# Starting the scatters of typed rows bank by bank, inside the stages that compute the rows

## The reference, cut to what matters

```python
x = _layernorm(x + _L2_gnn_ref(x, ...), axis=-1)
x = _layernorm(x + _L3_gnn_ref(x, node_type_16, edge_type_32, src, dst, ...), axis=-1)

def typed_linear(x, t, W):                      # each node by the matrix of its type
    y_all = jnp.einsum('nd,tdo->nto', x, W)     # 16 types
    return jnp.take_along_axis(y_all, t[:, None, None], axis=1)[:, 0]

def gt_layer(x, ntype, etype, src, dst, Wk, Wq, Wv, Wa, Watt, Wmsg, pri, skip, g, b):
    k, q, v = typed_linear(x, ntype, Wk), typed_linear(x, ntype, Wq), typed_linear(x, ntype, Wv)
    ...                                         # keys and values by edge type, scores, softmax, messages
    h = silu(typed_linear(hag, ntype, Wa))
    h = h * alpha + x * (1.0 - alpha)
    return (h - mean(h)) * rsqrt(var(h) + 1e-05) * g + b

h = x
for l in range(2):
    h = gt_layer(h, ...)
return h @ ff_w + ff_b
```

## Time and profile before

| | |
|---|---|
| Median of 3 runs | 6942.57 us (6941.76 to 6949.24) |
| The profiled execution's own time | 6940.74 us |
| Its span, in which all positions in the trace are told | 6937.9 us |
| Busy: TensorE, VectorE, ScalarE, GpSimd | 49%, 33%, 16%, 46% |
| Mean granted TensorE clock | 0.647 of full speed |

### The profile page before, as it was taken

The page is one execution under the profiler, slowest core; times in us unless marked ns, Lnnn a source line. Parts: engine busy times, 40 slices in busy tenths (PEclk is TensorE's granted clock), DMA queues, the critical chain, the costliest instruction groups (busy, mean ns, idle before and its releaser), DMA issues. The chain is left out here.

```text
span 6937.9 us, 64367 instructions
## 1 busy us (share of the span) xinstructions
PE 3401.2 (49%) x15913; PEld 2652.2 (38%) x15913; DVE 2282.3 (33%) x5027; ACT 1115.3 (16%) x2358; POOL 3195.3 (46%) x3405
## 2 busy tenths in 40 slices
PE   2566567646774555743363334633433446244344
PEld 2565445434453555532233232223333322233243
DVE  5222222222223222411121114523337535233385
ACT  0000122222222001200010001410103424011043
POOL 1666356635662565166636663045540230555302
PEclk8555577777776555655575556766666767566676
DMA  1111133323432232211131115954442479444333
GB/s 41 43 46 46 40 94 99 100 68 93 100 100 78 73 85 84 97 43 46 47 120 43 46 43 210 426 163 122 122 116 85 138 275 426 116 123 122 106 115 109
DMA packets 600942, 772.38 MB, mean 111 GB/s; under 512 B 89734, under 2 KB 507000, under 8 KB 588064
## 3 DMA queue, kind: packets, MB, share of 16 engines
q1 hardware_dynamic: 480000, 492.16, 21.3%
q0 software_dynamic: 120608, 276.12, 14.9%
HBM read 416.10 MB, written 351.82 MB: 111 GB/s over the span
## 5 line engine op out<-in xcount | busy, mean ns | idle before, releaser
L396 POOL DMA_INDIRECT arena<-table,idx_s x3128 | 2973.1, 950 | 2753.8 <-issue 867.9
L633 PE MATMUL ps<-arena,onehot 128*128 x4160 | 1067.3, 399 | 772.3 <-issue 483.1
L633 PEld LDWEIGHTS ps<-arena,onehot 128*128 128x128 f32 x4160 | 854.8, 284 | 921.0 <-issue 920.3
L374 DVE TENSOR_TENSOR onehot<-ps,dl_s 128x512 f32<-128x512 f32 x520 | 351.4, 686 | 1391.7 <-remote 1026.2
L1813 PE MATMUL ps<-ident,onehot 128*128 128x128 f32 x832 | 192.0, 374 | 658.4 <-DVE onehot L374 492.5
L1773 DVE TENSOR_TENSOR arena<-arena,ps 128x128 f32<-128x128 f32 x832 | 183.9, 282 | 845.2 <-remote 642.1
L803 DVE SCALAR_TENSOR_TENSOR arena<-ps,vecs,arena 128x256 f32<-128x256 f32 x208 | 100.6, 484 | 971.4 <-issue 617.2
L1824 PE MATMUL ps<-arena 128*128 x1664 | 330.5, 363 | 153.4 <-issue 108.7
L1813 PEld LDWEIGHTS ps<-ident,onehot 128*128 128x128 f32 x832 | 136.1, 194 | 688.8 <-DVE onehot L374 508.1
L1824 PEld LDWEIGHTS ps<-arena 128*128 128x128 f32 x1664 | 298.1, 269 | 182.7 <-issue 179.9
L1693 PE MATMUL ps<-arena,XT 32*128 32x512 f32 x1600 | 307.0, 900 | 97.1 <-DVE XT L1717 48.5
(11 more groups left out here) (327 smaller groups left out, 4520.8 us busy)
## 6 DMA issues: line engine op xcount, KB each, us to landing
table<-arena SPq DMA_DIRECT2D x96, 2048.0 KB
values<-arena SPq DMA_DIRECT2D x832, 64.0 KB
arena<-values SPq DMA_DIRECT2D x208, 256.0 KB
arena<-table,idx_s POOLq DMA_INDIRECT x3128
arena<-edge_times SPq DMA_DIRECT2D x208, 128.0 KB
edge_part<-arena SPq DMA_DIRECT2D x208, 128.0 KB
table<-arena SPq DMA_DIRECT2D x50, 512.0 KB
arena<-edge_part SPq DMA_DIRECT2D x98, 256.0 KB
```

The costliest lines, as they stand in the source:

```text
L374: is_dst = dve.tensor_tensor(onehot[:, 4 * q:4 * q + 4, :], iota.unsqueeze(1).to_broadcast([P, 4, P]), dl_s[:, ds(j, 4)].unsqueeze(2).to_b ...
L396: pool.indirect_dma_start(ring[:, ds(t % RING * 2 * H, width)], None, tab, bass.IndirectOffsetOnAxis(ap=idx_s[:, t:t + 1], axis=0)).then_i ...
L633: mm = pe.matmul(accf[:, ds(b, P)], o, ring[:, ds(slot, H)], start=False, stop=False, skip_group_check=True)
```

## The change

Four edits:

1. The scatters of the keys/values/queries product leave `by_type_phase`. For layer 0 they stand in the stage ahead of it, each bank of 4 behind a wait on `scaled`, and read `Xn`. For layer 1 they stand in the last stage of layer 0, behind that stage's 25 gathers, each bank behind a wait on `rows_ready`, which VectorE now raises in both layers.
2. The loads of weights, `Watt`, `Wmsg` and `pri` move with them, on semaphores of their own (`weighed`, `paired`). A few small tiles of the last stage get other places in `arena`, since the weights now lie where they stood.
3. `residual_norm_phase` and the small copying stage ahead of layer 0 become one stage. The addition, mean, squares and scaling are done bank by bank with the helpers that other stages use, and squares are summed on ScalarE.
4. The copy to `Lx` moves from GpSimd to ScalarE, bank by bank.

The typed product on the messages (`heard=True`) keeps its scatters and loads where they were.

```diff
-            residual_norm_phase(lambda ch, dve: ch(dve.tensor_tensor(Xn[:, :, :], Xn[:, :, :], acc_nodes, ALU.add)))
...
+            def place_rows(pool, src, b):
+                pool.indirect_dma_start(sorted_x, bass.IndirectOffsetOnAxis(ap=pos_i[:, b:b + 1], axis=0),
+                                        src[:, b, :], None).then_inc(placed.sem, 16)
+
+            def type_loads(sp, weights, layer):
+                C = len(weights) * H
+                wall = type_w[:, 0:NT * C].rearrange("p (t c) -> p t c", t=NT)
+                for w, W in enumerate(weights):
+                    sp.dma_start(wall[:, :, w * H:(w + 1) * H], W.rearrange("t f o -> f t o")).then_inc(weighed.sem, 16)
+                if layer is not None:
...
 def by_type_phase(src, weights, sorted_y, layer=None, heard=False):
-                    @block.gpsimd
-                    def _(pool):
-                        for b in range(NB):
-                            if heard and b % 4 == 0:
...
+                    if heard:
+                        @block.gpsimd
+                        def _(pool):
+                            for b in range(NB):
...
+                        if heard:
+                            type_loads(sp, weights, layer)
                         sp.wait_ge(placed.sem, placed.at(16 * NB))
...
                 if l == 0:
                     with nc.Block() as block:
+                        square = arena[:, 10000:10000 + NP].rearrange("p (b f) -> p b f", f=H)
+                        @block.sync
+                        def _(sp):
+                            type_loads(sp, kvq_weights[0], 0)
                         @block.gpsimd
                         def _(pool):
-                            pool.tensor_copy(Lx[:, :, :], Xn[:, :, :])
+                            for b in range(NB):
+                                if b % 4 == 0:
+                                    pool.wait_ge(scaled.sem, scaled.at(b // 4 + 1))
+                                place_rows(pool, Xn, b)
+                        @block.scalar
+                        def _(act):
+                            for k in range(BANKS):
+                                act_squares(act, k, Xn, k + 1, square)
+                            act_root(act, 1)
+                            for k in range(BANKS):
+                                c = slice(span(k)[2][0], span(k)[2][-1] + 1)
+                                act.wait_ge(scaled.sem, scaled.at(k + 1))
+                                act.activation(Lx[:, c, :], Xn[:, c, :], ACT.Copy)
                         @block.vector
                         def _(dve):
                             ch = Chain(dve, vdone)
+                            for k in range(BANKS):
+                                a, e, blocks = span(k)
+                                c = slice(blocks[0], blocks[-1] + 1)
+                                ch(dve.tensor_tensor(Xn[:, c, :], Xn[:, c, :], accf[:, a:e].rearrange("p (b f) -> p b f", f=H), ALU.add))
+                                dve_mean(ch, dve, k, Xn, red)
+                            dve_deviation(ch, dve, BANKS, 1)
+                            for k in range(BANKS):
+                                dve_scale(dve, k, Xn)
                             ch(dve.scalar_tensor_tensor(w1_f, src_s[:, 0:TILES], float(T32), t32_s[:, 0:TILES], ALU.mult, ALU.add))
                             ch(dve.tensor_copy(idx_s[:, 0:TILES], w1_f))
```

In the last stage of a layer, on GpSimd behind the 25 gathers, on SyncE behind the four small loads, and on VectorE per bank:

```diff
+                        if not last:
+                            for b in range(NB):
+                                if b % 4 == 0:
+                                    pool.wait_ge(rows_ready.sem, rows_ready.at(b // 4 + 1))
+                                place_rows(pool, Lx, b)
...
+                        if not last:
+                            type_loads(sp, kvq_weights[1], 1)
...
-                            if last:
-                                dve.sem_inc(rows_ready.sem, 1)
-                                if k >= 2:
-                                    output(k - 2)
+                            dve.sem_inc(rows_ready.sem, 1)
+                            if last and k >= 2:
+                                output(k - 2)
```

More of the change, by code:

```diff
@@ L190, in build @@
         produced = signal("produced")
+        weighed = signal("weighed")
+        paired = signal("paired")
         cube = arena[:, 0:STEPS * NB]
@@ L1514, in build @@
             join = arena[:, 20600:20600 + LINKS + 1]
[L1515 to L1518, removed]
+            alpha = arena[:, 23200:23200 + NB]
+            types_n = arena[:, 23240:23240 + NB].bitcast(I32)
+            skip_bc = arena[:, 23280:23280 + NT]
+            eq_types = arena[:, 23300:23300 + NB * NT].rearrange("p (b t) -> p b t", t=NT)
             vals = arena[:, 7600:7600 + U * H].rearrange("p (r f) -> p r f", r=U)
@@ L1535, in kvq @@
                 return arena[:, 18700 + (b - 16) * 3 * H:18700 + (b - 15) * 3 * H]
+            def place_rows(pool, src, b):
[7 more added lines that the diff above has]
+                if layer is not None:
+                    sp.dma_start(raw[:, 0, :, :].rearrange("p t o -> p (t o)"), A["L3_Watt"][layer]).then_inc(paired.sem, 16)
+                    sp.dma_start(raw[:, 1, :, :].rearrange("p t o -> p (t o)"), A["L3_Wmsg"][layer]).then_inc(paired.sem, 16)
+                    for h in range(HEADS):
+                        sp.dma_start(pri[h * HS:(h + 1) * HS, :], A["L3_gnn_pri"][layer, h].partition_broadcast(HS)).then_inc(paired.sem, 16)
             def by_type_phase(src, weights, sorted_y, layer=None, heard=False):
@@ L1543, in by_type_phase @@
                 extra = 2 + HEADS if layer is not None else 0
-                flat_src = src[:, :, :].rearrange("p b f -> p (b f)")
+                flat_src = src[:, :, :].rearrange("p b f -> p (b f)") if heard else None
                 with nc.Block() as block:
-                    @block.gpsimd
-                    def _(pool):
-                        for b in range(NB):
-                            if heard and b % 4 == 0:
[L1550 to L1553, removed]
+                    if heard:
[3 more added lines that the diff above has]
+                                if b % 4 == 0:
+                                    k = b // 4
+                                    pool.wait_ge((mixed if k % 2 == 0 else squared).sem, (mixed if k % 2 == 0 else squared).at(k // 2 + 1))
+                                place_rows(pool, src, b)
                     @block.sync
                     def _(sp):
[L1557 to L1563, removed]
+                        if heard:
+                            type_loads(sp, weights, layer)
                         sp.wait_ge(placed.sem, placed.at(16 * NB))
@@ L1589, in _ @@
                         turn(0)
-                        pe.wait_ge(loaded.sem, loaded.at(16 * len(weights)))
+                        pe.wait_ge(weighed.sem, weighed.at(16 * len(weights)))
                         for g in range(GROUPS):
@@ L1623, in _ @@
                             ch(dve.tensor_reduce(pair_mask, head_mask[:, :].rearrange("p (a j) -> p j a", j=2), AX.X, ALU.add))
-                            dve.wait_ge(stored.sem, stored.at(16 * extra))
+                            dve.wait_ge(paired.sem, paired.at(16 * extra))
                             ch(dve.tensor_tensor(raw[:, 0, :, :], raw[:, 0, :, :], pri.unsqueeze(2).to_broadcast([P, T32, HS]), ALU.mult))
@@ L1637, in _ @@
                             dve.tensor_copy(out_ring[:, g % 6, c, :], ps[:, 2 + n % 6, 0:C]).then_inc(copied.sem, 1)
-                loaded.base += 16 * len(weights)
-                stored.base += 16 * extra
+                weighed.base += 16 * len(weights)
+                paired.base += 16 * extra
                 placed.base += 16 * NB
@@ L2021, in build @@
             for l in range(2):
+                kvq_weights = [[A["L3_gnn_Wk"][n], A["L3_gnn_Wv"][n], A["L3_gnn_Wq"][n]] for n in range(2)]
                 if l == 0:
                     with nc.Block() as block:
+                        square = arena[:, 10000:10000 + NP].rearrange("p (b f) -> p b f", f=H)
+                        @block.sync
+                        def _(sp):
+                            type_loads(sp, kvq_weights[0], 0)
                         @block.gpsimd
                         def _(pool):
-                            pool.tensor_copy(Lx[:, :, :], Xn[:, :, :])
+                            for b in range(NB):
[11 more added lines that the diff above has]
+                                act.activation(Lx[:, c, :], Xn[:, c, :], ACT.Copy)
                         @block.vector
@@ L2034, in _ @@
                             ch.close()
-                by_type_phase(Lx, [A["L3_gnn_Wk"][l], A["L3_gnn_Wv"][l], A["L3_gnn_Wq"][l]], sorted_kvq, layer=l)
+                    for s in (centred, squared, scaled):
+                        s.base += BANKS
+                    for s in (varied, rooted):
+                        s.base += 1
```

(2 more changed lines are left out.)

## The result

The changed kernel takes **6928.8 us** (median of 15 runs, 6911.3 to 6939.1), the kernel before, run beside it, 6947.2 us (15 runs, 6934.6 to 6958.1): a ratio of 0.9975, 95% interval 0.9967 to 0.9983, that is 12 to 23 us less. The forecast was 6916 us with a range of 6911 to 6928, so the measured median lies 0.8 us above that range.

The account below looks back on a forecast made before the run. No engine is busy over 49%; at both seams GpSimd's scatter issuing is on the path and starts late. 13.4 + 13.6 - 0.5 = 26.5 us gained, from 6942.57 to 6916 us; range 6911 to 6928 for 8 in 10.

Parts of the forecast that it names:

- Start of the scatters, layer 0: Ahead of layer 0: with the norm done by banks, GpSimd gets bank 0 and starts scattering 13.4 us earlier.
- Start, layer 1: Between the layers: the first scatter follows the first Lx bank by 0.1 us, 13.6 us earlier.
- Pace of the scatters: Both seams: scatters beside VectorE's short instructions slow slightly, 1.1 us net, ends 0 and 2.1; 0.5 us taken as lost.
- The end of the stage: Both seams: the meeting of all engines behind the last scatter is covered by the scatter's 1.29 us landing, costing 0.
- the 27.0 at the start of the sum: Both seams: the earlier scatter starts, 13.4 us and 13.6 us, before the 0.5 us lost in pace.
- TensorE's registers and VectorE's tables: After the meeting at each seam: loading 40 tile types and making tables cost 0, at most 1 us each.
- The loads moved: Last stage of layer 0: early weights delay gathers of the first three banks, which are caught up; cost 0.
- The port rival: Both seams: VectorE's unbroken scaling rows keep GpSimd from the shared ports; gain 15.5 us, time 6927; chance 0.12.
- The gather rival: Layer 0's last stage: early weights delay the gathers, banks finish at 5543.5 against 5539.81; gain 22.8, time 6920; chance 0.12.
- The clock rival: Layers behind the seams: TensorE's granted clock falls to 0.66, products stretch 50 us, time 6966; chance 0.05.
- The entry rival: Next stage's entry: TensorE's registers or first instructions come 1 to 3 us late per seam; gain 20 to 24; chance 0.08.
- The tests named ahead: Changed profile: first scatter 13.4 us after norm's start, 25 scatters 31.5 to 33 us, seams gaining 20 us, layers within 5.

Follow-up runs that it names:

- experiment 6: Changed kernel and the version without meetings of engines, each beside the kernel before: 5802.0 us and 5800.0 us against 5823.8 us.
- Experiment 4: Changed kernel with both sets of scatters back at the typed product's start, loads still early: one run, 6967.9 us against 6953.7 for the kernel before.
- Experiments 1 and 2: 1: changed kernel without meetings of engines, 6924.9 us, ratio 0.9974; 2: changed kernel with a GpSimd drain between gathers and scatters of second seam, 6917.2 us, ratio 0.9965.
- Experiment 5: Changed kernel with the loads back at the typed product's start, scatters still early: 6969.3 us, ratio 1.0023 to the kernel before.

## Why the prediction was wrong

The direction, the place of the gain and the earlier start of the scatters were right. One wait was put at nothing and is on the path, and the gain came out too large. The forecast of 6916 misses 6928.8 by 12.8 us, in three parts:

- **5.2 us: the seams gained 21.3 and not 26.5.**
- **4.6 us: the starting point.** The three runs shown gave before 6942.57 us, fifteen give 6947.19. Single runs of one kernel lie up to 18 us from their median here (6911.3 against 6928.8), and the upper end of the range had nothing for that.
- **3.0 us: the rest**, between the seams' 21.3 and the medians' 18.4. It lies within the interval of 12 to 23 us, and in the runs of experiment 6, with less scatter, it isn't there.

Step by step:

- *Start of the scatters, layer 0* (13.4): 13.15. Right. Experiment 4 shows that 5.7 us of the seam is owed to the norm and the merged stage without any early scatter.
- *Start, layer 1* (13.6): 12.93. The root was 0.44 us later, and the first scatter came 0.33 us behind the bank where 0.1 was taken.
- *Pace of the scatters* (0.5 lost): nothing lost, 31.98 and 32.03 us. The slowest is 1.36 us, beside the index instruction of 392 columns; beside scaling none passes 1.14.
- *The end of the stage* ("it is covered: 0"): **the step that failed.** SyncE was to be released by the landing, 1.29 us after the last scatter, with the meeting hidden under it; instead the meeting waited for GpSimd's drain. It cost 1.27 us at the first seam and 3.10 at the second, 4.4 of the 5.7 us that the seams fell short of the 27.0 at the start of the sum. The price of a meeting was taken from the earlier trace rows, where the last work ahead of it was a GpSimd copy, not an indirect DMA. A row for the first seam was there to be read: the drain in the typed product's stage, 2.3 us past its last scatter. It cost nothing there, so no list of waits showed it, and the change moved it onto the path. Experiments 1 and 2 confirm it from two sides: the load comes 1.3 us behind the last scatter without a meeting, and 2.6 with the gathers drained before.
- *TensorE's registers and VectorE's tables* (0, at most 1 each): load to TensorE 3.07 us at both seams, where before had 2.65 and 3.09. 0.4 us in all.
- *The loads moved* (0): right in the main, and by its reason. Bank 0 was 3.5 us late, and six later banks caught it up but for the 0.44 us above; in other traces with early weights the root is up to 1.8 us late, and once 5.5. Experiment 5 prices the alternative.
- *The port rival* (0.12) is false: first scatters take 1.00 and 1.03 us. *The gather rival* didn't come about here: the root is 0.4 us later, where it had 3.7 (in the traces of experiments 4 and 2 it was 1.8 and 5.5 later). *The clock rival* is false: the layers behind changed by -1.8 and +3.4 us where it had 50, and the granted clock over each is 0.68 against 0.69. *The entry rival* (gain 20 to 24) had the right size by luck, with a wrong cause: what is late is not an instruction of the next stage but the end of the one before.

The tests named ahead held but for some tenths of a microsecond, with seams over 20 us and layers equal within 5 (though the layers vary by more than that from trace to trace), except one: from the last scatter's end to TensorE 3.9 to 4.5 us were forecast, and 5.6 and 7.5 came. That test points at the failed step.

## What to carry to other kernels

When work moves across a meeting of all engines, ask of each engine what its drain will cost at the new place, and read it from the sequencers' own rows: a drain that nobody waited for appears in no list of waits. Move what the next stage reads together with what releases it; here early scatters with late weights made the seams 8 us longer, and early weights alone gained nothing at the second seam. And where the gain is the size of one run's scatter, measure the seam in the trace, and put the median's own uncertainty in the range.

## What the runs showed of the hardware

**GpSimd's drain outlasts its indirect DMAs, and by more after more of them.** After 25 scatters it ends 2.3 us after the last one's row does, after 25 gathers 2.5 to 2.6; after 50 of them without a drain between 4.2 us. With a drain between them SyncE runs again 2.6 us after the last, as it does after 25. It isn't the landing, on which a semaphore releases SyncE 1.3 us after the row. The Trainium skill (DMA: Bandwidth & Descriptors, section Anatomy of one DMA — SWDGE (gpsimd) path) gives such a DMA about 2.0 us plus its bytes at 436 GB/s, an estimate of 2.15 us for 64 KB; from a scatter's start to SyncE's release are 0.97 + 1.29 = 2.26 us, so the trace agrees. The growth isn't in proportion to the count. In the kernel before, the stages with 391 gathers close with a DRAIN that lasts 9.1 us, though it begins only after the last gather has ended (4149.95 at the last of these five):

```profile
L568 POOLq DRAIN  x5: 9112/9112/9120, 707.4 to 4152.8; - x5
```

It costs nothing there either: the other engines end later, and the norm's first addition follows at 4171.65. Why the drain grows was not tried.

**Two-input VectorE instructions do hold up a gather.** The stretch ahead of the earlier trace rows in the kernel before, first VectorE's timeline, then GpSimd's:

```profile
2942.90 3.62 DVE L1192 TENSOR_TENSOR link<-arena 128x3328 f32<-128x3328 f32 x1
2946.56 3.62 DVE L1193 SCALAR_TENSOR_TENSOR link<-arena,link 128x3328 f32<-128x3328 f32 x1
...
2952.98 3.62 DVE L1198 TENSOR_REDUCE arena<-link 128x1 f32<-128x3328 f32 x1
```

```profile
2943.80 3.54 POOL L396 DMA_INDIRECT arena<-table,idx_s  x1 [0.30 <-issue]
2947.64 3.35 POOL L396 DMA_INDIRECT arena<-table,idx_s  x1 [0.30 <-issue]
...
2955.32 0.95 POOL L396 DMA_INDIRECT arena<-table,idx_s  x1 [0.30 <-issue]
```

Both slow gathers end 0.8 us after the VectorE instruction beside them does, as in the earlier trace rows; beside the TENSOR_REDUCE a gather takes its usual 0.95. The Trainium skill (SBUF — State Buffer, section Who interferes with whom) infers that `tensor_tensor` leaves descriptor generation alone; these rows show otherwise.

**Weights delay gathers at first, and little in the end.** 3.6 MB issued beside 25 gathers made the first bank 3.5 us late and the seventh 0.4 us (37.73 us after the first gather against 37.29). In the other traces the first bank is 3.1 to 3.6 us late too, and the root between 0.1 and 1.8 us, once 5.5 us.
